# Carrying an eviction into the next block, and three moves beside it, in a routed mixture-of-experts kernel

## What is computed

```python
x = L0_attn_x                                    # (2, 2048, 256)
x = _layernorm(x + ssm(x))                       # diagonal state space layer
# the feed-forward part, on 4096 tokens, 8 experts, 4 of them per token, H = 682
gate = einsum('bsd,ed->bse', x, Wg) + routing_bias
weights = softmax over the 4 largest gates, 0 elsewhere
out = _swiglu(x, Ws1, Ws2, Ws3)                  # the shared expert: every token
h1 = einsum('bsd,ehd->ebsh', x, W1); h2 = einsum('bsd,ehd->ebsh', x, W2)
eo = einsum('ebsh,edh->ebsd', sigmoid(h1) * h1 * h2, W3)
out = out + einsum('ebsd,bse->bsd', eo, weights)
x = _layernorm(x + out)
```

## Time and profile before

| | us |
|---|---|
| three runs | 1052.86, 1055.35, 1060.98 (median 1055.35) |
| the profiled execution | 1057.69 |
| its span from first to last instruction | 1055.9 |
| mean granted TensorE clock | 0.987 |

### The profile page before, as it was taken

How to read it: one execution, slowest core, us unless ns; L and a number is a source line. 1 busy time by engine, 2 the same in 40 slices (tenths; PEclk the granted TensorE clock), 3 DMA queues, 4 the chain that set the end, 5 groups by cost and what they waited for, 6 DMA issues and landing times.

```text
span 1055.9 us, 27243 instructions
## 1 busy us (share of the span) xinstructions
PE 990.5 (94%) x8620; PEld 839.6 (80%) x8621; DVE 592.9 (56%) x1680; ACT 524.7 (50%) x1367; POOL 532.4 (50%) x501
## 2 busy tenths in 40 slices
PE   7997989999999999989889989999999999999985
PEld 3556868888887888878778878878888888888864
DVE  3998897546544444544544545454454545454677
ACT  2665644445554554544534545454454545554455
POOL 3464055348233335823855025075678764675662
PEclk9998999999999999999989999999999999999999
DMA  7856133533633233353234124128673675766674
GB/s 230 215 131 164 21 79 87 157 83 92 171 101 97 84 96 102 86 166 97 62 124 138 44 51 125 46 50 182 102 110 63 106 108 88 117 102 96 84 145 111
DMA packets 167876, 113.83 MB, mean 108 GB/s; under 512 B 113421, under 2 KB 160016, under 8 KB 166673
## 3 DMA queue, kind: packets, MB, share of 16 engines
q0 software_dynamic: 30480, 59.41, 26.3%
q1 hardware_dynamic: 115088, 32.33, 15.3%
q10 hardware_dynamic: 22256, 21.50, 5.9%
HBM read 47.09 MB, written 40.96 MB: 83 GB/s over the span
## 4 chain that ended last, share of the span: by engine, by line
PE 44%; DMA 26%; POOL 9%; DVE 8%; issue 8%; ACT 3%; SPq 1%; ACTq 0%; POOLq 0%; DVEq 0%
PE psA L981 29%; DMA rows_by_place<-y_rows,place 23%; PE psB L1006 11%; POOL rows_by_place L656 3%; POOL work L586 2%; PE psA L932 2%; POOL work L579 1%; POOL stage L580 1%; PE psC L963 1%; DVE stat L1403 1%; PE psB L1009 1%; ACT y_sum L892 1%; SPq L492 1%; ACT sil L813 1%; DMA rows_by_place<-zeros,pad_at 1%
## 5 line engine op out<-in xcount | busy, mean ns | idle before, releaser
L813 ACT ACTIVATE sil<-psA 128x256 f32<-128x256 f32 (+1 forms) x510 | 188.1, 374 | 304.8 <-PE psA L981 248.2
L1311 DVE SCALAR_TENSOR_TENSOR g<-psA,sil 128x256 f32<-128x256 f32 (+1 forms) x178 | 73.6, 414 | 319.8 <-ACT sil L813 301.6
L700 POOL DMA_INDIRECT y_sum<-rows_by_place,place x128 | 198.5, 1551 | 103.7 <-DMA y_sum<-rows_by_place,place 79.5
L981 PE MATMUL psA<-xb_odd,work 128*128 128x256 f16 x2112 | 238.1, 274 | 10.5 <-issue 7.2
L656 POOL DMA_INDIRECT rows_by_place<-y_rows,place x128 | 128.8, 1006 | 226.4 <-DMA rows_by_place<-y_rows,place 179.9
L981 PE MATMUL psA<-xb,work 128*128 128x256 f16 x2046 | 231.9, 275 | 10.1 <-DMA row_weights<-rows_by_place 6.7
L981 PEld LDWEIGHTS psA<-xb_odd,work 128*128 128x128 f16 x2112 | 206.2, 98 | 39.8 <-issue 15.2
L981 PEld LDWEIGHTS psA<-xb,work 128*128 128x128 f16 x2046 | 200.3, 99 | 38.2 <-issue 12.8
L1006 PE MATMUL psB<-work,g_hi 128*128 128x256 f16 x1320 | 220.7, 273 | 1.9 <-DVE g_lo L1321 1.5
L1311 DVE SCALAR_TENSOR_TENSOR psC<-psA,sil 128x256 f32<-128x256 f32 (+1 forms) x332 | 140.2, 422 | 93.0 <-ACT sil L813 76.6
L1006 PE MATMUL psB<-work,g_lo 128*128 128x256 f16 x660 | 179.9, 273 | 0.0
(11 more groups left out here) (154 smaller groups left out, 841.4 us busy)
## 6 DMA issues: line engine op xcount, KB each, us to landing
stage<-wpack POOLq DMA_DIRECT2D x9, 2176.0 KB, 8.8
rows_by_place<-eb ACTq DMA_DIRECT2D x63, 256.0 KB
work<-xT SPq DMA_DIRECT2D x8, 512.0 KB, 4.9
work<-half_beta SPq DMA_DIRECT2D x8, 512.0 KB, 4.7
work<-x_tok POOLq DMA_DIRECT2D x8, 512.0 KB, 6.0
rows_by_place<-y_rows,place POOLq DMA_INDIRECT x128, 2.5
y_sum<-rows_by_place,place POOLq DMA_INDIRECT x128
out<-y_sum ACTq DMA_DIRECT2D x4, 512.0 KB
```

What stands on the lines that cost most here:

```text
L700: pool.indirect_dma_start(out=y_sum[:, n, :], out_offset=None, in_=xs, in_offset=bass.IndirectOffsetOnAxis(ap=place[:, k, n:n + 1], axis=0 ...
L813: act.activation(sil[r0:r0 + n, c % SLOTS, 0:T], psA[0:n, c % HVS, 0:T], ACT.Silu, scale=1.0 / (XS * WS)).then_inc(silu_ready, 1)
L981: last = pe.matmul(dst, W[:, ws, k, ci, :], xb[slot][:, KD * xs_ + k, 0:T], start=(k == 0 and n == 0), stop=(k == KD - 1 and n == 2))
L1311: dve.scalar_tensor_tensor(gated_rows(g, c, 0, n, T), src, 1.0 / (XS * WS), sil[r0:r0 + n, c % SLOTS, 0:T], ALU.mult, ALU.mult).then_inc(g ...
```

## The change

It has four parts. (1) ACT evicts an expert block within the next block: behind that block's first silu, with the two stores (one per 128 rows, instead of one per block) behind its second silu and first `high`. What to evict is carried in registers (`carry`): an offset into one weight tile and two row numbers. Block 0 evicts a block that is multiplied with zeros and stored into two spare groups behind the rows (`SINK`), and a half block's empty half goes there too. A half block now uses the second bank of `psB`. In an ACT block the work `beside` a chunk comes after its silu and `high`, not before. (2) The routing weights get their own semaphore, so PE waits for the transposes alone. (3) Eight of the twelve steps of expert 3's conversion go behind scatters 24 to 31 of rank 3, four behind `pad_rows(3)`. (4) `finish` is split: `moments` stays between the blocks, the roots (`inverse`) go behind the next block's first gating; ACT's normalisation is spread over four chunks instead of five.

```diff
@@ SP, load_rows
-                if J < JB:
-                    sp.sem_inc(xb_loaded, 16)
-                counted(sp, down_read, S1 + b)
+                sp.sem_inc(xb_loaded, 16 * (JB - J + 1))
+                counted(sp, down_read, S1 + b + 1)
+                counted(sp, row_weights_loaded, 16 * b + 16)
                 r0 = nc.s_assert_within(sp.snap(group * P), 0, (NG - J) * P)
-                sp.dma_start(row_weights[slot][:, :, :],
-                             xs[bass.ds(r0, T), D:RW].rearrange("(j p) e -> p j e", p=P)).then_inc(xb_loaded, 16)
+                sp.dma_start(row_weights[:, slot, JB - J:JB, :],
+                             xs[bass.ds(r0, T), D:RW].rearrange("(j p) e -> p j e", p=P))\
+                    .then_inc(row_weights_loaded, 16)
@@ POOL
-            scatter(3, 0, convert_beside(2, 1, 16))
+            second_set = convert_beside(2, 1, 16)
+            third = conversion(4)
+            THIRD_FROM = 24
+            def rank_3_beside(n):
+                second_set(n)
+                if n == THIRD_FROM:
+                    counted(pool, down_ready, blocks_until(pool, 1) + S1)
+                if n >= THIRD_FROM:
+                    convert_step(third, 4, 1, n - THIRD_FROM)
+            scatter(3, 0, rank_3_beside)
             pool.wait_ge(pads_written[2], 16)
             pad_rows(3)
+            for i in range(NT - THIRD_FROM, 2 * len(pieces)):
+                convert_step(third, 4, 1, i)
...
                 if 1 <= e < E - 2:
-                    counted(pool, down_ready, done + S1)
-                    convert(e + 3, e % 2)
+                    if e > 1:
+                        counted(pool, down_ready, done + S1)
+                        convert(e + 3, e % 2)
...
-                    counted(pool, rows_stored, done * 16 + 16)
+                    counted(pool, rows_stored, (done + 1) * 16 * JB + 16)
@@ ACT
+            def evict_carried(b):
+                w0 = act.snap(carried_weights, min_val=0, max_val=(NO_ROWS * JB + 1) * E - 1 - E)
+                act.wait_ge(row_weights_loaded, 16 * b + 16)
+                act.wait_ge(down_read, b + S1 + 1)
+                act.wait_ge(down_ready, b + S1)
+                act.wait_ge(rows_stored, 16 * JB * b + 16)
+                for j in range(JB):
+                    last = act.activation(eb[:, j, :], psB[:, j, 0:D], ACT.Copy,
+                                          scale=weight_at[:, bass.ds(w0 + j * E, 1)])
+                last.then_inc(down_read, 1)
+            def store_carried(b):
+                act.wait_ge(down_read, b + S1 + 2)
+                for j in range(JB):
+                    r0 = act.snap(carried_rows[j], min_val=0, max_val=(NG + SINK - 1) * P)
+                    act.dma_start(xs[bass.ds(r0, P), 0:D], eb[:, j, :]).then_inc(rows_stored, 16)
@@ ACT, ffn_block
                 if ahead:
                     ahead()
+                if carried is not None:
+                    evict_carried(carried)
                 for c in range(first, NC):
-                    if beside:
-                        beside(c - 1)
                     if ahead:
...
                         silu(c)
                         high(c - first)
+                    if beside:
+                        beside(c - 1)
+                    if carried is not None and c == 1:
+                        store_carried(carried)
@@ ACT, the blocks
             def expert_rows(e, T, b, group, slot):
-                ffn_block(b + S1, T)
...
+                ffn_block(b + S1, T, carried=b)
+                last = act.snap((group + T // P - 1) * P)
+                carry(slot * JB * E + e, [act.snap(group * P) if T == TB else NG * P, last])
...
-                ffn_block(r + S1 + i, beside=None if lot is None else lambda c: norm_groups(lot, c, NC - 1))
+                ffn_block(r + S1 + i, beside=None if lot is None else lambda c: norm_groups(lot, c - 1, NC - 2) if c else None,
+                          carried=None if i else r)
@@ PE, down
-                pe.wait_ge(down_read, g + 1)
+                pe.wait_ge(down_read, g + (1 if isinstance(g, int) else 2))
...
-                        o = psB[:, j, 0:D]
+                        o = psB[:, JB - T // P + j, 0:D]
@@ DVE, ffn_block and the last blocks
                     gated(c)
+                    if c == 0 and first:
+                        first()
...
-                ffn_block(g, beside=by_pool if lot and LOTS.index(i - 1) == POOL_LOT else None)
+                ffn_block(g, beside=by_pool if lot and LOTS.index(i - 1) == POOL_LOT else None,
+                          first=(lambda: inverse(LOTS.index(i - 2), FINISH[i - 2])) if i - 2 in LOTS else None)
                 if lot and LOTS.index(i - 1) != POOL_LOT:
                     gathered(max(ORDER.index(q) for q in lot))
-                    counted(dve, down_read, g + 1)
-                    finish(LOTS.index(i - 1), lot)
+                    counted(dve, down_read, g + 2)
+                    t.add(moments(LOTS.index(i - 1), lot))
```

More of the change, by code:

```diff
@@ L109, in build @@
     RW = D + E
-    xs = nc.dram_tensor("rows_by_place", [NG * P, RW], F32, kind="Internal").ap()
+    SINK = 2
+    xs = nc.dram_tensor("rows_by_place", [(NG + SINK) * P, RW], F32, kind="Internal").ap()
     xs_values = xs[:, 0:D].bitcast(F16)
@@ L203, in build @@
         eb = sb("eb", [P, JB, D], F32)
-        row_weights = ([sb(f"row_weights{n}", [P, JB, E], F32) for n in range(2)]
-                       + [sb(f"row_weights_odd{n}", [P, JB, E], F32) for n in range(2)]
-                       + [sb(f"row_weights_half{n}", [P, 1, E], F32) for n in range(2)])
+        NO_ROWS = 6
+        row_weights = sb("row_weights", [P, NO_ROWS + 1, JB, E], F32)
+        weight_at = row_weights[:, :, :, :].rearrange("p s j e -> p (s j e)")
         nmv = [sb(f"nmv{n}", [P, 8, 2], F32) for n in range(2)]
@@ L266, in build @@
         xb_loaded = sem("xb_loaded")
+        row_weights_loaded = sem("row_weights_loaded")
         spare_filled = sem("spare_filled")
@@ L302, in build @@
         wdi = sm[:, OW:SM].rearrange("p (m w k e) -> p m w k e", m=KD, w=2, k=KD)
-        NCONST = 13
+        NCONST = 14
         steps = range(NSTEP)
@@ L531, in _ @@
             pool.memset(gate_room[:, :, E:GW], PAST).then_inc(consts_ready, 1)
+            pool.memset(row_weights[:, 4:NO_ROWS + 1, :, :], 0.0).then_inc(consts_ready, 1)
             pool.memset(best[:, :, K:8], PAST).then_inc(consts_ready, 1)
@@ L539, in _ @@
             pool.sem_inc(rows_stored, 16)
+            pool.sem_inc(row_weights_loaded, 16)
             pool.wait_ge(small_loaded, 16)
@@ L804, in last_rows, with carry, ffn_block @@
                 turned(NSTEP - 1)
-            def ffn_block(g, T=TB, ahead=None, beside=None):
+            carried_weights, *carried_rows = (nc.alloc_registers(f"carried_{name}", engines=[act.engine])
+                                              for name in ("weights", "row0", "row1"))
+            def carry(weights, rows):
+                nc.regs_mov(carried_weights, weights)
+                for regs, row in zip(carried_rows, rows):
+                    nc.regs_mov(regs, row)
+            def evict_carried(b):
[13 more added lines that the diff above has]
+                    act.dma_start(xs[bass.ds(r0, P), 0:D], eb[:, j, :]).then_inc(rows_stored, 16)
+            def ffn_block(g, T=TB, ahead=None, beside=None, carried=None):
                 def silu(c):
@@ L874, in _ @@
             act.wait_ge(blocks_ready, 1)
+            carry(NO_ROWS * JB * E, [(NG + j) * P for j in range(JB)])
             for e in range(E):
@@ L1303, in first_low, with ffn_block @@
                         dve.tensor_copy(lo[r:end, full:m], hi[r:end, full:m]).then_inc(first_low_ready, 1)
-            def ffn_block(g, T=TB, beside=None, later=None):
+            def ffn_block(g, T=TB, beside=None, later=None, first=None):
                 def gated(c):
@@ L1408, in moments, with inverse @@
                 return ins
-            def finish(lot, pairs):
-                t.add(moments(lot, pairs))
+            def inverse(lot, pairs):
                 groups = [y[:, q * JB + j, :] for q in pairs for j in range(JB)]
@@ L1449, in by_pool @@
                     gathered(max(ORDER.index(q) for q in lot))
-                    counted(dve, down_read, g + 1)
+                    counted(dve, down_read, g + 2)
                     moments(POOL_LOT, lot).then_inc(pool_moments_ready, 1)
-                ffn_block(g, beside=by_pool if lot and LOTS.index(i - 1) == POOL_LOT else None)
+                ffn_block(g, beside=by_pool if lot and LOTS.index(i - 1) == POOL_LOT else None,
+                          first=(lambda: inverse(LOTS.index(i - 2), FINISH[i - 2])) if i - 2 in LOTS else None)
                 if lot and LOTS.index(i - 1) != POOL_LOT:
                     gathered(max(ORDER.index(q) for q in lot))
-                    counted(dve, down_read, g + 1)
-                    finish(LOTS.index(i - 1), lot)
```

(7 more changed lines are left out.)

5 lines of the change are left out of this document (3 added, 2 removed).

## The result

The changed kernel takes 1062.95 us (median of 20 runs, 1057.82 to 1069.24) beside 1055.56 for the kernel before (20 runs, 1050.06 to 1062.87). The ratio is 1.007, 95% interval 1.0052 to 1.0087: slower by 0.7%, some 7 us. The forecast was 1052.0, faster by 0.3%, with a range of 1045 to 1058. Measured again with the later experiments, the ratio was 1.0073.

A forecast was written before the change was run, and what follows sets the result against it. PE was taken as the bound, busy 990.5 of 1055.9 us. Conversion -7.0, half blocks +2.4 and the end +1.2 (waits +2.0, late blocks -0.8) sum to -3.4: from the median 1055.35 to 1052.0 us, range 1045 to 1058.

The forecast's parts named there:

- Part 1, full blocks: Full expert blocks: eviction and one more DMA issue on ACT between first and third silu cost PE nothing, 0 us.
- Part 1, half blocks: Six half blocks: eviction and two store issues delay the third silu, +0.4 us each, +2.4 us in all.
- Part 2, the semaphore: PE's gaps before even experts: dropping the wait for routing weights changes nothing, 0 us.
- Part 3, the conversion: Expert 3: conversion ends at 520.4, the stall shrinks from 5.75 to 0.96 and up keeps the clock, -7.0 us.
- Part 4: Last four shared blocks: later roots, with silus and first high done by then, gain 0.2 us each, -0.8 us.
- The end: After the last expert block: later store starts rank 3's gathers about 4 us later, waits of 0.8 and 1.2, together +2.0 us.
- B: Rival: ACT's carried work costs more than conversion gains; half blocks +1.0 each, last store +3.0; 1057.4 us, chance 0.12.
- A: Rival: half blocks 0.5 us shorter each, no gather wait, two full blocks keep the clock; 1041.3 us, chance 0.14.
- C: Rival: scatters beside expert 3's conversion wait longer, pads, SP's load and PE come late; gain 2, 1057 us, chance 0.08.
- the signs listed as proof of being wrong: Half blocks moving over 0.8 us, the end shrinking over 2 us, or a gap appearing in full blocks.

The follow-up runs named there:

- TensorE's instruction: Kernel before with only one more PE register instruction per block, the high_doubled semaphore starting at one and its wait asking one more: 1.0040.
- the added matmuls: 36 more 128x256 matmuls in down of the last block ahead of the experts: 1.0004 on the kernel before, 0.9979 on that with expert 3's conversion moved.
- the register shared: Changed kernel with the high_doubled semaphore started at one, so down's two waits compare with the same value and the added register instruction is gone: 0.9985.
- the last store at once: Changed kernel with the last expert block evicted and stored ahead of the first late shared block: 1.0027; with both down waits also at one value: 1.0004.
- carrying: Kernel before with only the carried eviction and its own semaphore, down's two waits at one value, last expert block evicted and stored at once: 1.0004.

## Why the prediction was wrong, and where it was right

Each line holds the differences between runs that differ by one edit, in per cent of the kernel before. Each is uncertain by some 0.3 to 0.4:

| edit | differences |
|---|---|
| third | -0.5 and -0.6 alone, -0.6 beside the fourth, -0.3 beside TensorE's instruction, -0.25 beside the added matmuls, -0.4 and -0.2 with the eviction carried and the register shared, +0.2 in the changed kernel |
| TensorE's instruction | +0.4 alone, +0.6 and +0.7 beside the third, +0.9, +0.3 and +0.2 in forms of the changed kernel |
| fourth | +0.4 alone, +0.2 and +0.3 beside the third, +0.2 with the last store at once |
| late last store | +0.4, and -0.2 with the shared register |
| carrying | 0.0 alone, +0.3 and +0.45 beside the third |

Only the first three keep their side in nearly every pair. A sum of one value from each line can be made to meet the measured +0.7, but so can others, so the sum explains nothing by itself. What stands best is the instruction: without it the changed kernel is at 0.9985 [0.9954, 1.0017], some 1054 us and inside the range, though not clear of no change; with it the kernel is slower.

- **Part 1, full blocks (0).** This is the step that failed. "I take 0. Above, PE would show a gap of its own in up" was right for ACT, and up shows no gap. But it looked for the cost in waits and not in the instructions that compute their values. The carried eviction raises down's wait for `down_read` by one. That split a shared register and made PE's sequencer late at every second block boundary: 2.5 us in 38 quiet blocks, and 0.2 to 0.9% in all, the largest single cost.
- **Part 1, half blocks (+0.4 each).** Too high: from start to start the five that do not lie before expert 3 changed by -0.03 to +0.14 each. The second DMA issue costs ACT its 0.43 (0.88 for two against 0.45), but up no longer stalls and the time reappears in down. Here the Trainium skill's sentence that a sequencer's issue is small beside the DMA (DMA: Bandwidth & Descriptors, Issuing engines are not separate DMA queues) gave the better number: by it the half blocks come out even, and they did.
- **Part 2, the semaphore (0).** Right as far as it goes: PE's gaps before even experts did not shrink (2.55 and 2.17 against 2.26 and 2.13).
- **Part 3, the conversion (-7.0).** Right at the place: pads at 511.9 (511.5 forecast), conversion over at 521.0 (520.4), and 6.9 us gained at expert 3 in the third edit alone. That the pads met the forecast within 0.5 is partly luck, since over the twelve profiles with the edit they start at 504.3 to 515.2. The sum left out the blocks beside the steps, up to 2.6 us, and the next weights, now fetched 8.3 us earlier into the transposes, by which the gap came out at 2.04 and not 0.96 in the changed kernel. It also took the stall of one execution, 4.8 us, as the kernel's. In four of seven profiles it wasn't there.
- **Part 4 (-0.8).** Wrong in sign: +0.4 to +0.9. The block with six groups did gain, 0.15 in the mean (13.26 to 13.11), but the last block loses 0.46 to the two groups ahead of its last high row.
- **The end (+2.0 for the waits).** Mechanism right, size short in most profiles. The gathers start 4.4 us later after PE's first late matmul (about 4 forecast). The five kernels with the late store lose 0.4 to 5.9 in the last block but one, 3.1 in the mean. The lag of the first gather (6.4 to 8.7 us) and the gathers' pace (2.25 to 2.41 us over rank 3) both vary.
- **The rivals.** B had the side and half of the mechanism: the last store at +3.0 is near what the profiles show, the half blocks at +1.0 are not. A is out: the half blocks did not shrink. C is out for the third edit alone; in the changed kernel its outcome came, no gain from part 3, with SP's load late as it said, but with the place itself still gaining. None named PE's own instructions, and of the signs listed as proof of being wrong none came.

## What to carry to other kernels

A change to a wait's value is a change to the instruction stream of the engine that waits: compare the register operations of the two kernels on the bounding engine before calling it free. Before pricing a stall, ask whose time it stands on, and look at it in more than one execution: where two engines race, the later one sets the start, and the stall of one profile can be gone in the next. When you add work to test such a place, check that no wait ahead of it swallows the work first. A store that is moved behind other work matters only where it is the last of its chain; there, leave it where it was.

## What was not expected of the hardware

A register instruction on PE's sequencer shows up although no gap is listed: the two matmul rows around the loop's branch move from 0.23 to 0.39 us apart. And the same gap does not always cost the clock. Before an even expert the changed kernel has the row at 630.38, shown above, with a gap of 2.17, and this one:

```profile
760.66 0.61 PE L1025 MATMUL psA<-xb,work 128*128 128x256 f16 x4 [2.17 <-DMA xb<-rows_by_place]
```

After the first the block takes 10.99 us; after this one 12.38, with a granted clock of 0.86 over it. From the first expert block to the start of the last block the time lost to the clock (length times one minus the granted clock) adds up to between 1.7 and 9.8 us from one profiled execution to the next, with no tie to an edit that I could find. It is why a single profile could not have settled steps of 0.4%.
